# f1 and f2 per node by TensorE from the turned x, normalisation split over ScalarE, VectorE and GpSimd, in the preamble of a graph attention and Mamba kernel

## What is computed

```python
x = layernorm(x)                       # (x - mean) / sqrt(var + eps), per node
feat_1 = x @ a[:F]                     # f1, one number per node
feat_2 = x @ a[F:]                     # f2, one number per node
e = leaky_relu(feat_1 + feat_2.T, 0.2)
U = softmax(where(adj > 0, e, -9e15), axis=1)
prop_u = U @ x
```

## Time and profile before

| | before |
|---|---|
| median of 3 runs | 787.05 us |
| the profiled execution, its own time | 786.87 us |
| its span, first to last instruction | 785.1 us |
| mean granted TensorE clock | 0.991 |
| busy share PE, DVE, ACT, POOL | 94%, 93%, 85%, 81% |

### The profile page before, as it was taken

How to read it: one execution, slowest core, us unless ns; L and a number is a source line. 1 busy time by engine, 2 the same in 40 slices (tenths; PEclk the granted TensorE clock), 3 DMA queues, 4 the chain that set the end, 5 groups by cost and what they waited for, 6 DMA issues and landing times.

```text
span 785.1 us, 21076 instructions
## 1 busy us (share of the span) xinstructions
PE 741.4 (94%) x6049; PEld 708.5 (90%) x6049; DVE 726.4 (93%) x1898; ACT 671.1 (85%) x1428; POOL 632.7 (81%) x1215
## 2 busy tenths in 40 slices
PE   3689999999999999987899999999999999999987
PEld 1378999999999999977899999999999999999975
DVE  6999999999999999797999999999989899989986
ACT  5999898999899898955888888888889898989865
POOL 5583788888888888886888888888888888888863
PEclk9989999999999999999999999999999999999999
DMA  7689898989898986022221212121212121210000
GB/s 218 187 258 316 288 298 272 313 276 343 260 324 283 307 286 239 18 66 68 68 65 46 68 45 68 43 67 43 67 46 67 44 69 41 70 42 18 10 4 15
DMA packets 97961, 110.43 MB, mean 141 GB/s; under 512 B 6865, under 2 KB 89713, under 8 KB 97905
## 3 DMA queue, kind: packets, MB, share of 16 engines
q1 hardware_dynamic: 97906, 109.78, 43.3%
HBM read 90.87 MB, written 18.89 MB: 140 GB/s over the span
## 4 chain that ended last, share of the span: by engine, by line
PE 73%; DVE 13%; POOL 7%; issue 3%; ACT 2%; DMA 1%; POOLq 0%; DVEq 0%; ACTq 0%
PE accA L1701 26%; PE accC L1710 25%; DVE code L777 4%; PE ps L1640 3%; PE ps L1808 3%; PE ps L1792 3%; PE ps L1825 2%; DVE maskC L785 2%; PE ps L1806 2%; PE ps L1790 2%; PE ps L1810 2%; PE ps L1844 2%; PE ps L1817 1%; PE ps L1827 1%; DVE Y L756 1%
## 5 line engine op out<-in xcount | busy, mean ns | idle before, releaser
L1338 ACT ACTIVATE maskA<-code 128x1024 fp32r<-128x1024 int8 x256 | 269.2, 1053 | 20.7 <-DVE code L777 17.6
L1701 PE MATMUL accA<-Y,maskA 128*128 128x260 f32 (+1 forms) x1792 | 270.0, 293 | 1.7 <-issue 1.6
L1710 PE MATMUL accC<-Y,maskC 128*128 128x260 f32 (+1 forms) x1792 | 253.2, 284 | 4.3 <-DVE maskC L785 4.3
L1701 PEld LDWEIGHTS accA<-Y,maskA 128*128 128x128 f32 x1792 | 232.3, 191 | 4.6 <-issue 2.2
L1710 PEld LDWEIGHTS accC<-Y,maskC 128*128 128x128 f32 x1792 | 228.9, 189 | 5.6 <-DVE maskC L785 5.5
L785 DVE TENSOR_SCALAR maskC<-code 128x1024 fp32r<-128x1024 int8 x256 | 206.1, 806 | 0.1
L777 DVE SCALAR_TENSOR_TENSOR code<-f_rows,neg_f,ps 128x512 int8<-128x512 int8 (+1 forms) x256 | 178.2, 739 | 1.7 <-PE ps L1640 0.5
L1275 ACT ACTIVATE edges<-adj_in 128x1024 int8<-128x1024 f32 x128 | 135.3, 1059 | 2.0 <-DMA adj_in<-in_adj_dram 2.0
L638 POOL TENSOR_TENSOR room_r<-room,room_r 128x256 fp32r<-128x256 f32 x128 | 97.7, 791 | 2.5
L1063 DVE SCALAR_TENSOR_TENSOR room<-room 128x128 f32<-128x128 f32 x270 | 86.2, 340 | 0.0
L1640 PE MATMUL ps<-ident,edges 128*128 128x128 bf16 x512 | 51.2, 224 | 10.0 <-ACT edges L1275 10.0
(11 more groups left out here) (275 smaller groups left out, 1624.0 us busy)
## 6 DMA issues: line engine op xcount, KB each, us to landing
adj_in<-in_adj_dram SPq DMA_DIRECT2D x128, 512.0 KB, 5.0
edge_codes<-code SPq DMA_DIRECT2D x32, 512.0 KB, 5.6
code<-edge_codes SPq DMA_DIRECT2D x32, 512.0 KB, 3.3
xn<-in_x_dram SPq DMA_DIRECT2D x4, 512.0 KB, 5.7
room<-in_x_dram SPq DMA_DIRECT2D x32, 64.0 KB, 1.8
room<-in_L_gnn_h_dram SPq DMA_DIRECT2D x32, 64.0 KB, 2.0
out_dram<-room SPq DMA_DIRECT2D x32, 64.0 KB, 1.6
room<-in_L_ffn_W_in_dram SPq DMA_DIRECT2D x1, 192.0 KB, 2.5
```

Source lines behind the costliest of these rows:

```text
L1338: s.activation(maskA[:, b % MASKS], src, ACT.Relu, bias=1.0 - LINK, scale=-1.0).then_inc(S["maskA_ready"], 1)
L1701: t_.matmul(accA[k][:, 0:2 * cols], maskA[:, b % MASKS, l * P:(l + 1) * P], y2_of(jt, 0) if cols == F else Y[:, jt, 0, :, 0:cols], start=j ...
L1710: m = t_.matmul(accC[k][:, 0:2 * cols], maskC[:, b % MASKS, l * P:(l + 1) * P], y2_of(jt, 1) if cols == F else Y[:, jt, 1, :, 0:cols], sta ...
```

## The change

f2 is no longer made on VectorE. For each quarter, once its turned x is copied to `xnT`, TensorE multiplies each of its four tiles (as stationary operand) by a 128 by 2 matrix `a_cols` that holds both halves of `a`, and so gets f1 and f2 with a node per partition in PSUM. VectorE copies them out per chunk (`columns`), with -f2 beside it. The trip of f1 through DRAM, its two transfers in SyncE's queue, its transpose and the broadcast load of `a` go. The normalisation is split anew: ScalarE chunks 0 and 1, VectorE chunk 2, GpSimd chunk 3. The copies of the turned x are shared, even quarters by ScalarE and odd ones by VectorE. The maximum over f2 now comes after jt 2, `biases` after jt 3, the square of colw after jt 5 and the low part of the columns after jt 8.

```diff
-            sp.dma_start(a2_row, a[F:2 * F].rearrange("f o -> o f").broadcast_to([P, F])).then_inc(S["small_in"], 16)
-            sp.dma_start(a_col[:], a[0:F]).then_inc(S["small_in"], 16)
+            for side in range(2):
+                sp.dma_start(a_cols[:, side:side + 1], a[side * F:(side + 1) * F]).then_inc(S["small_in"], 16)
...
+            for t in range((XCH - 1) * TPC, NT):
+                g.tensor_scalar(xn[:, t, :], xn[:, t, :], mv[:, t, 0:1], rstd[:, t:t + 1], ALU.subtract, ALU.mult).then_inc(S["norm_late"], 1)
...
-                    v.tensor_tensor_reduce(f2_prod[:, t], xn[:, t, :], a2_row, 1.0, 0.0, ALU.mult, ALU.add, f2col[:, t:t + 1]).then_inc(S["dots_done"], 1)
...
+            def turned_copy(q):
+                dve.wait_ge(S["xT_done"], q + 1)
+                v.tensor_copy(xnT[:, q * 512:(q + 1) * 512], accA[q % 2][:, :]).then_inc(S["xT_moved"], 1)
+
+            def columns(k):
+
+                mine = slice(k * TPC, (k + 1) * TPC)
+                dve.wait_ge(S["f12_made"], k + 1)
+                both = ps[2 + k % 2][:, 0:2 * TPC].rearrange("p (t c) -> p t c", c=2)
+                v.tensor_scalar(neg_f2[:, mine], both[:, :, 1], -1.0, None, ALU.mult).then_inc(S["negf_ready"], 1)
+                v.tensor_copy(f12[:, :, mine].rearrange("p c t -> p t c"), both).then_inc(S["f12_copied"], 1)
...
-            dots(0)
-            normalise(XCH - 1)
-            for k in range(1, XCH):
-                dots(k)
...
+            turned_copy(1)
+            normalise(2)
+            turned_copy(3)
+            columns(0)
+            turned_copy(5)
...
+                if jt == 0:
+                    turned_copy(7)
                 if jt == 1:
+                    columns(1)
+                if jt == 2:
+                    columns(2)
+                    columns(3)
+                    dve.wait_ge(S["f12_copied"], XCH)
+                    v.tensor_reduce(grow[:, 5:6], f2col, AX_X, ALU.max).then_inc(S["fmax_done"], 1)
+                if jt == 3:
                     biases()
...
+            def columns(q):
+
+                k = q // 2
+                pe.wait_ge(S["xT_moved" if q % 2 else "xT_copied"], q // 2 + 1)
+                if q % 2 == 0 and k >= 2:
+                    pe.wait_ge(S["f12_copied"], k - 1)
+                for t in range(q * 4, q * 4 + 4):
+                    m = t_.matmul(ps[2 + k % 2][:, 2 * (t % TPC):2 * (t % TPC) + 2], xnT[:, t * P:(t + 1) * P], a_cols[:], start=True, stop=True)
+                if q % 2:
+                    m.then_inc(S["f12_made"], 1)
...
             f1_matmul(0)
+            pe.wait_ge(S["small_in"], 32)
+            columns(0)
             turn_x(2)
+            columns(1)
             turn_x(3)
+            turn_x(4)
+            columns(2)
+            turn_x(5)
+            columns(3)
             turn(0, 0, first=True)
+            columns(4)
+            turn_x(6)
+            columns(5)
+            turn_x(7)
             turn(0, 1, first=True)
-            for q in range(4, NT // 4 - 1):
-                turn_x(q)
+            columns(6)
+            columns(7)
+            pe.wait_ge(S["f12_copied"], 3)
+            turn(0, 2, first=True)
+            pe.wait_ge(S["f12_copied"], XCH)
             pe.wait_ge(S["fmax_done"], 1)
```

More of the change, by code:

```diff
@@ L101, in gnn_ffn_kernel @@
         ones = sb("ones", [P, P])
-        a_col = sb("a_col", [P, 1])
+        a_cols = sb("a_cols", [P, 2])
         early, featsum, hcol = shared("early", [P, F + NT * 6], F32, [("featsum", [P, 2, F], F32), ("hcol", [P, 2, NT], F32)])
-        a2_row = early[:, 0:F]
         stats = early[:, F:F + NT * 6].rearrange("p (t c) -> p t c", c=6)
         a1_wide = sb("a1_wide", [P, P])
-        f1_tiles = a1_wide[0:NT, :]
         col_mean = sb("col_mean", [P, F])
@@ L480, in _ @@
                     g.tensor_tensor(shift_mean[:, mine], shift_mean[:, mine], rstd[:, mine], ALU.mult).then_inc(S["rstd_done"], 1)
-                else:
-                    g.tensor_tensor(rstd[:, mine], rstd[:, mine], consts[:, 0, mine], ALU.pow).then_inc(S["rstd_done"], 1)
+                elif k == 2:
+                    g.tensor_tensor(rstd[:, mine], rstd[:, mine], consts[:, 0, mine], ALU.pow).then_inc(S["rstd_done"], 1)
+                else:
+                    link(g.tensor_tensor(rstd[:, mine], rstd[:, mine], consts[:, 0, mine], ALU.pow))
+            for t in range((XCH - 1) * TPC, NT):
+                g.tensor_scalar(xn[:, t, :], xn[:, t, :], mv[:, t, 0:1], rstd[:, t:t + 1], ALU.subtract, ALU.mult).then_inc(S["norm_late"], 1)
             end_chain()
@@ L717, in normalise @@
                 for t in range(k * TPC, (k + 1) * TPC):
[L718 to L726, removed]
-                    v.tensor_tensor_reduce(f2_prod[:, t], xn[:, t, :], a2_row, 1.0, 0.0, ALU.mult, ALU.add, f2col[:, t:t + 1]).then_inc(S["dots_done"], 1)
+                    v.tensor_scalar(xn[:, t, :], xn[:, t, :], mv[:, t, 0:1], rstd[:, t:t + 1], ALU.subtract, ALU.mult).then_inc(S["norm_mid"], 1)
+            def turned_copy(q):
[7 more added lines that the diff above has]
+                v.tensor_copy(f12[:, :, mine].rearrange("p c t -> p t c"), both).then_inc(S["f12_copied"], 1)
             for k in range(XCH):
@@ L775, in codes @@
                 dve.wait_ge(S["tr_done"], n + 1)
+                if isinstance(G, int) and G == 0:
+                    dve.wait_ge(S["negf_ready"], jt // TPC + 1)
                 rows = bass.ds(v.snap(G * 512) if not isinstance(G, int) else G * 512, 512)
@@ L1292, in _ @@
             normalise(1)
-            turned_copy(1)
-            normalise(2)
+            turned_copy(2)
             f1_copy(0)
             sign(0, 0, first=True)
+            turned_copy(4)
             sign(0, 1, first=True)
-            for q in range(2, 5):
-                turned_copy(q)
+            turned_copy(6)
             sign(0, 2, first=True)
-            turned_copy(5)
-            turned_copy(6)
             sign(0, 3, first=True)
             act.wait_ge(S["bias_ready"], 1)
-            s.activation(colw[:, 0, :, 0], f2col[:], ACT.Exp, bias=grow[:, 7:8])
-            s.activation(colw[:, 1, :, 0], f2col[:], ACT.Exp, bias=grow[:, 5:6], scale=SLOPE).then_inc(S["colw_done"], 1)
-            turned_copy(7)
+            s.activation(colw[:, 0, :, 0], f2col, ACT.Exp, bias=grow[:, 7:8])
+            s.activation(colw[:, 1, :, 0], f2col, ACT.Exp, bias=grow[:, 5:6], scale=SLOPE).then_inc(S["colw_done"], 1)
             sign(0, 4)
```

46 lines of the change are left out of this document (16 added, 30 removed).

## The result

| | before | after |
|---|---|---|
| median of the runs on one chip | 787.71 us (786.87 to 789.63, 4 runs) | 800.24 us (798.61 to 803.06, 4 runs) |
| profiled execution, its own time | 786.87 us | 799.40 us |
| its span | 785.1 us | 797.6 us |
| milestone: codes 0 to 3 and biases done | 28.12 us | 37.98 us |
| handover: first maskC behind the preamble | 60.65 us | 73.11 us |

The change makes the kernel slower: the ratio of the times is 1.0159, 95% interval 1.0123 to 1.0196. That is 12.5 us. The direction was forecast, the size was not: 791.5 us was predicted, with a range that ends at 798.5.

What follows compares the result with a forecast made beforehand. VectorE's list was taken to bound the preamble up to the handover to TensorE. Milestone 3.5 us later, then -0.3 + 0.95 + 0.3, gave 4.4 on 786.87, 791.3; with 0.2 for the median 791.5 us, range 786.8 to 798.5.

Steps and rivals of the forecast that it cites:

- The serial end: End of the preamble: from VectorE's copy of quarter 7 at 26.25 us through columns, maximum and spread to biases at 31.65.
- rival "faster": Narrow matmuls on TensorE cost far less than the weight-load pace, records at 0.055: 782.4 us, chance 0.11.
- The wait in y_low_a: Behind the milestone: VectorE, done with code 7 at 35.6, waits 0.95 us for ScalarE's high part of Y.
- Here I let the clock rise at 19.0: TensorE's chain in the preamble: higher clock level from 19.0 us, so transposes cost 0.5 and four tiles of columns 0.9.
- The clock stays low through the preamble: Rival for TensorE's preamble: two moving columns leave the array mostly idle; 9.2 us more, 800.7 us, chance 0.16.
- A record of columns at the low level: TensorE's column matmuls: 0.25 us apart at the lower level, so four tiles cost 2.0 us.
- The milestone with the clock as I had assumed it: Codes 0 to 3 and biases done at 31.65 us against 28.12, 3.5 us later.
- GpSimd's normalisations: Eight of 128x128 take 4 us from 16.4, ending at 20.4; rival that they are late: 797.5 us, chance 0.04.
- X6: TensorE's four transposes of quarter 6 in the preamble, forecast at 24.15 us; 0.5 high, 0.85 low.
- the rows' version: VectorE's normalisations run unhindered beside GpSimd's powers and end near 16.6 us, against 18.5 if a power blocked them.
- From the milestone to the handover: Later part of the preamble: 0.3 us less lost in the square, 0.95 more in y_low_a, 0.3 more in low columns.
- the meetings: Big VectorE instructions beside GpSimd's long ones: six meetings of up to 2.4 us, put at plus or minus 2.5.

Runs made afterwards that it cites:

- wide64: The changed kernel with the moving operand of columns 64 wide instead of 2: 794.15 us, ratio 1.0099 to the kernel before.
- quarter: The changed kernel with one matmul of 8 columns per quarter of x in place of four of 2, output not the reference's: 788.67 us, ratio 1.0022.
- warm: The changed kernel with 18 idle 128x128 products on TensorE ahead of the first transposes: 799.41 us, ratio 1.0168.
- wide_warm: The changed kernel with 64 moving columns and 18 idle products ahead of the first transposes: 791.62 us, ratio 1.0069.
- all: wide_warm with the edits of late_low and columns_early, and the second f1 matmul ahead of the last columns: 786.81 us, ratio 1.0011.
- late_low: wide_warm with VectorE's first y_low_a and first maskC moved from behind jt 7 to behind jt 9: 788.42 us, ratio 1.0025.
- columns_early: wide_warm with VectorE's small copies of the columns taken earlier: 791.81 us, ratio 1.0051.

## Why the prediction was wrong in size

**What held.** The handover is where the preamble's price is paid: from there to the end of the span it is 724.0 to 725.2 us in all twelve profiles. VectorE, freed of the dots, waits for TensorE. The serial end (copy of quarter 7, columns, maximum, spread, biases) is as told. At the higher level the records of columns are 0.105 apart in wide64, where the earlier trace rows gave 0.10 to 0.112. Four records of 8 columns take 0.58 in quarter (at 24.52), against 0.56 for four of 64, which fits a pace set by the weight load. So the rival "faster" by records of 0.055 is out, though no run has records of two columns at that level. The wait in y_low_a is 1.30 us, forecast 0.95.

**The step that failed** is the sentence "Here I let the clock rise at 19.0 (the rows leave 17.6 to 21.4)". Those rows were of a kernel whose TensorE did an f1 matmul and transposes of 128 columns and then rested; I carried the rise over to one that spends most of its time on two columns. It came after 38 us. wide64 measures what this costs: 7.6 us at the milestone, and 5.1 in the span or 6.1 in the median. And I had stopped reading too early: even in the kernel before the higher level didn't last. The earlier trace rows is of 26 us; between 21.4 and that its trace has

```profile
22.00:24.00 2.00, 1.68 (x10) 0.50 0.60 157
22.79 2.74 PE L1657 MATMUL accA<-ident,xn 128*128 128x128 f32 x12
```

The clock had fallen again near 22, and these transposes are 0.21 apart, the low level, up to 25 us. The forecast had everything from 19.0 on at the higher one. My own rival "The clock stays low through the preamble" gave 800.7, against 800.24 measured; that it hangs on the two moving columns is what wide64 bears out, and I gave the whole case 0.16. The argument against it, that the clock "rose in 17.6 to 21.4 after a weaker stretch", counted busy time, and left out the fall behind 21.4. warm shows what counting busy time is worth: 2.00 us busy in each 2, and a granted 0.50.

The Trainium skill ("TensorE: Matmul & The Clock Gate", section "What's actually happening") says that the low level is the default and activity releases it. The 421 ns ahead of the first change agree with the first half. For the second half, a TensorE that the trace records as busy throughout was not enough in warm.

**Terms that were mis-sized.**
- A record of columns at the low level: taken as 0.25 from sums of 128 columns, measured 0.196. With the 0.25 the rival has the milestone at 31.65 + 9.2 = 40.85, and it was 37.98. That the rival's total was right to 0.5 us is partly luck: the later part, below, made up 1.65 of those 2.9 us, and the median stood 0.8 above the profiled execution, not 0.2.
- The milestone with the clock as I had assumed it: wide64 gives 30.4 where I said 31.65. Forecast as 3.5 behind before, it is 2.3. Quarter 7's transposes end 1.7 earlier (24.35) than the 26.05 of the forecast: the f1 matmul begins at 13.42, not 13.9 (the load of x, forecast as 0.3, gave more), the first columns take 1.59, not 2.0, and the rise comes at 17.7. The serial end is then 0.45 longer, partly at the low level again.
- GpSimd's normalisations: "8 x 0.5 = 4 us", measured 6.24, 0.78 each, to 22.6. In after it costs nothing, X6 comes later; in quarter, wide_warm and all it is a wait of 0.3 to 1.3 us. GpSimd's timeline of after, beside the earlier trace rows:

```profile
14.59 1.66 POOL L473 TENSOR_TENSOR rstd<-rstd,consts 128x8 f32<-128x8 f32 x1
16.37 6.24 POOL L475 TENSOR_SCALAR xn<-xn,mv,rstd 128x128 f32<-128x128 f32 x8
```

- The power at 14.59 lies beside VectorE's eight normalisations of 14.33 to 16.47, and these take 2.14 us, as they did with nobody beside them. So the rows' version was right and the power doesn't block. The Trainium skill ("SBUF — State Buffer", section "Terms") says that the port pair which VectorE and GpSimd share is held for the full instruction. The trace agrees for the long ones: low columns of 128 elements take 1.79 us beside a GpSimd instruction of 1024 elements (47.64 to 50.44) and 0.28 alone. Beside the power it shows no hold-up.
- From the milestone to the handover: 0.95 + 0.3 - 0.3 in the forecast, 2.6 measured.

This last one can be read in full from VectorE's timelines, in us (six: the four y_low_a and the two maskC ahead of the handover, summed):

| | before | after | wide64 | wide_warm | late_low |
|---|---|---|---|---|---|
| wait in y_low_a | 0 | 1.30 | 1.46 | 1.47 | 0 |
| low columns | 0.69 | 1.79 | 1.78 | 1.33 | 0.28 |
| square of colw | 1.76 | 1.40 | 1.41 | 1.41 | 1.41 |
| the six | 12.03 | 12.30 | 14.64 | 12.02 | 11.61 |
| milestone to handover | 32.5 | 35.1 | 37.4 | 34.3 | 32.2 |

Before to after: 1.30 + 1.10 - 0.36 + 0.27 = 2.3 of the 2.6. Before to wide64: 1.46 + 1.09 - 0.35 + 2.61 = 4.8 of 4.9. My "plus or minus 2.5" for the meetings was the right size; in after they cost 0.27 in the six and 1.1 in the low columns, which I had at 0.3. wide64 and wide_warm, equal up to the milestone, differ by 2.6 in the six. 1.6 of it is the first y_low_a, beside GpSimd's products. In wide64 it starts 0.13 behind them:

```profile
35.77 4.74 POOL L486 TENSOR_TENSOR code<-xn,colw 128x1024 f32<-128x1024 f32 x2 [0.87 <-PE accC L1645]
35.90 2.85 DVE L748 TENSOR_TENSOR Y<-ywork,Y 128x1024 fp32r<-128x1024 f32 x1 [1.46 <-ACT Y L1313]
```

and in wide_warm 0.17 ahead of them:

```profile
35.77 1.23 DVE L748 TENSOR_TENSOR Y<-ywork,Y 128x1024 fp32r<-128x1024 f32 x1 [1.47 <-ACT Y L1313]
35.94 5.12 POOL L486 TENSOR_TENSOR code<-xn,colw 128x1024 f32<-128x1024 f32 x2 [1.17 <-PE accC L1645]
```

So a shift of 0.3 us between two engines is worth 1.6 us here. Small moves in the order can swing the total by a us or two in this way.

**The change part by part, then.** Of the 12.5 us, 7.6 are what two columns cost against 64, by the clock; 2.3 are the chain of transposes and columns as it stands in wide64, with its wait of 1.5 for VectorE's copy and a low clock at both ends; and 2.6 are the later part. all takes back all of them in its shorter runs, and arrives at the time of before in the median.

## What to carry to other kernels

When a change moves work onto TensorE as many matmuls of a few columns, cost the whole stretch at the low clock level too, and try a padded moving operand: here 64 columns took hardly longer than 2 at the low level (1.59 against 1.56 us for eight records), and the kernel was 5 to 6 us faster. Read the level from the length of a known instruction, not from the granted clock ahead of its first change. Follow the clock in the rows to the end of the stretch that you forecast: a rise can be followed by a fall, as near 22 us in the kernel before. And a freed engine is only worth what its supplier can deliver: 6.9 us of dots went, and 14.9 us of waiting came.

## What was not expected of the hardware

- TensorE, recorded as busy 2.00 us in every 2 from 14 to 30 us, stood at a granted 0.50 there while its work was groups of two-column matmuls (1.57 us) between groups of transposes (0.88 or 1.74) (warm). The same matmuls with 64 columns were at the higher level from 17.7 to 28 us (wide64); in columns_early they began low too and rose near 20.
- A float32 record with a new 128x128 stationary operand is 0.196 us apart at the low level and 0.105 at the high one, with 64 columns as with 2 at the low one (1.59 and 1.56 for eight).
- VectorE's y_low_a of 1024 elements took 1.23 us when it started 0.17 us ahead of GpSimd's products (wide_warm), and 2.85 when it started 0.13 behind them (wide64).
- One normalisation of 128x128 took 0.78 us on GpSimd and 0.27 on VectorE (eight in 2.14).
